# Grouped attentions of a four-layer transformer kernel: the pair of scores goes to TensorE ahead of the pair of transposed scores

## The reference, cut to what matters

```
scores = einsum('hbqd,hbkd->hbqk', q, k) / sqrt(16)     # causal ones: -inf above the diagonal
p = softmax(scores, axis=-1)
a = einsum('hbqk,hbkd->hbqd', p, v)
```

## Time and profile before

| | |
|---|---|
| median of 3 runs | 1981.44 us |
| the profiled execution, its own time | 1984.31 us |
| its span in the trace | 1982.5 us |
| granted TensorE clock, mean | 0.925 of 2.4 GHz |
| TensorE (PE) busy | 1670.2 us, 84% |
| VectorE (DVE) busy | 1185.9 us, 60% |
| ScalarE (ACT) busy | 977.1 us, 49% |
| GpSimd (POOL) busy | 471.6 us, 24% |

### The profile page before, as it was taken

How to read it: one execution, slowest core, us unless ns; L and a number is a source line. 1 busy time by engine, 2 the same in 40 slices (tenths; PEclk the granted TensorE clock), 3 DMA queues, 4 the chain that set the end, 5 groups by cost and what they waited for, 6 DMA issues and landing times. The chain is left out here.

```text
span 1982.5 us, 29923 instructions
## 1 busy us (share of the span) xinstructions
PE 1670.2 (84%) x10912; PEld 1007.5 (51%) x10912; DVE 1185.9 (60%) x2606; ACT 977.1 (49%) x1547; POOL 471.6 (24%) x546
## 2 busy tenths in 40 slices
PE   5899999989999999931289999869998999998676
PEld 2455555568865565511145555546775344433443
DVE  3576767442335665649857666446444677775376
ACT  1677879732323555533025445536663366566322
POOL 5120210022323223011132321015664323210100
PEclk9899999999998999975589999978999899999698
DMA  6342240010043355010155325031112354140322
GB/s 205 78 96 49 65 94 4 1 64 0 0 126 105 97 149 149 2 49 0 40 149 149 95 74 132 1 121 48 49 49 83 90 149 136 46 117 1 115 85 86
DMA packets 67045, 156.16 MB, mean 79 GB/s; under 512 B 9869, under 2 KB 15382, under 8 KB 66010
## 3 DMA queue, kind: packets, MB, share of 16 engines
q1 hardware_dynamic: 66906, 154.32, 27.8%
HBM read 104.86 MB, written 51.52 MB: 79 GB/s over the span
## 5 line engine op out<-in xcount | busy, mean ns | idle before, releaser
L995 DVE TENSOR_REDUCE a_mx<-PS 128x1 f32<-128x512 f32 (+3 forms) x768 | 394.5, 552 | 195.1 <-PE PS L1237 118.5
L1178 ACT ACTIVATE a_pT<-PS 128x1024 f32<-128x1024 f32 (+3 forms) x384 | 308.7, 811 | 221.9 <-PE PS L1261 152.9
L1232 PE MATMUL PS<-a_k,a_q 64*128 64x512 f32 (+3 forms) x768 | 231.1, 420 | 34.3 <-DVE a_mx L995 24.5
L367 DVE CUSTOM_DVE_ANT_0 PS<-PS,a_dist 128x448 f32<-128x448 f32 x256 | 155.1, 648 | 73.7 <-PE PS L598 72.8
L1252 PE MATMUL PS<-a_q,a_k 64*128 64x512 f32 (+3 forms) x768 | 176.8, 440 | 12.0 <-DVE a_q L1000 6.2
L1275 PE MATMUL PS<-a_pT,a_va 128*32 128x512 f32 (+3 forms) x1536 | 168.6, 511 | 6.0 <-ACT a_raw L1136 6.0
L1232 PEld LDWEIGHTS PS<-a_k,a_q 64*128 64x128 f32 x768 | 107.4, 190 | 107.4 <-DVE a_mx L995 88.2
L498 ACT ACTIVATE a_p<-PS,a_negm 128x448 f32<-128x448 f32 (+1 forms) x256 | 149.2, 639 | 2.5 <-DVE a_negm L367 0.7
L608 PE MATMUL PS<-cst,a_p 128*128 128x128 f32 x1024 | 145.1, 285 | 4.7 <-DVE a_pT L376 2.0
L122 PE MATMUL PS<-cst 128*128 128x512 f32 x202 | 104.4, 647 | 43.9 <-PEq L66 36.7
L1252 PEld LDWEIGHTS PS<-a_q,a_k 64*128 64x128 f32 x768 | 78.5, 188 | 113.9 <-issue 88.3
(11 more groups left out here) (344 smaller groups left out, 3461.3 us busy)
## 6 DMA issues: line engine op xcount, KB each, us to landing
spread_scratch<-a_high SPq DMA_DIRECT2D x96, 256.0 KB, 7.1
a_q<-spread_scratch SPq DMA_DIRECT2D x96, 256.0 KB, 5.7
a_k<-spread_scratch SPq DMA_DIRECT2D x96, 256.0 KB, 6.6
f_gb<-gate_rows SPq DMA_DIRECT2D x68, 256.0 KB, 5.4
spread_scratch<-a_low SPq DMA_DIRECT2D x48, 256.0 KB, 7.5
window_scratch<-a_high SPq DMA_DIRECT2D x24, 256.0 KB, 2.3
a_q<-window_scratch SPq DMA_DIRECT2D x32, 192.0 KB, 5.8
a_k<-window_scratch SPq DMA_DIRECT2D x32, 192.0 KB, 6.3
```

The lines of the kernel that those rows point to most:

```text
L367: dve.tensor_tensor_reduce(PS[:, bank, 0:KW], PS[:, bank, 0:KW], dt_[:, off:off + KW], float(slopes[2 * pair + a]), 3e38, ALU.add, ALU.min ...
L995: dve.tensor_reduce(mx[:, gg % 2, qt, 2 * half + a:2 * half + a + 1], PS[:, 4 + a, 0:kw], AX.X, ALU.max).then_inc(max_done, 1)
L1178: act.activation(pT[:, N // 2 % 2, N % 2, :, q0:S], PS[:, 2 * (N % 2):2 * (N % 2) + 2, q0:S], ACT.Exp, scale=SCALE).then_inc(exp_done, 1)
L1232: mm = pe.matmul(ps[:, 0:kw], q[rows, b % 2, pair, qt * P:(qt + 1) * P], k[rows, b % 2, pair, 0:kw], start=True, stop=not causal)
```

## The change

In the loop over N of TensorE's order the pair of `scores` is put ahead of `scores_T(N)`. Nothing else is changed; no instruction, wait or buffer is added or removed, and the other engines keep their orders.

```diff
@@ -1357,10 +1357,10 @@
                 for u in range(NU):
                     pe.wait_ge(unit_low[u], 1)
                 for N in range(FULL):
-                    scores_T(N)
                     for t in (2 * N + LEAD, 2 * N + LEAD + 1):
                         if t < NB * TILES_:
                             scores(t)
+                    scores_T(N)
                     if N % 2 and N >= 3:
                         values((N - 3) // 2)
                     piece(*piece_at(N), previous_piece(N))
```

## The result

The changed kernel took 1991.14 us, the median of 12 runs (1986.11 to 2002.83), and before, run beside it 12 times, 1976.55 us (1970.60 to 1983.08): the ratio is 1.008 with a 95% interval of 1.0058 to 1.0101, so 14.6 us slower. The forecast was a sum of +14.5 us. The total is right, in part by luck: of its four terms two hold and two are too large, and a gain and many small costs that I had not seen make up the difference.

What follows compares the result with a forecast made beforehand. TensorE was taken to bound the attentions, in a ring of waits with VectorE. Terms 3.8 + 4.0 + 3.7 + 3.0 = +14.5 us on 1981.44 gave 1996 us; range for 8 in 10, 1974 to 2012.

Steps and rivals of the forecast that it cites:

- The ring: Scores, VectorE's reduction, scores after next in the same bank: same work as before in attention 3, so worth nothing.
- The copy of the finished group: Values after N % 8 = 2 wait for ScalarE's copy, 0.24 us later in 16 of 28 groups: +3.8 us.
- The division: At N % 8 = 3 VectorE's division delays the reduction; 0.30 lost less 0.14 gained, in 25 groups: +4.0 us.
- The rotations: Attention 2's twelve rotated pieces hold VectorE; transposed pairs of 0.24 to 0.40 us land behind the wait: +3.7 us.
- The widths: Behind the copy of the maxima, N % 8 = 0 gets a narrower filler, 0.16 us in 19 groups: +3.0 us.
- theory B: The experiments' alternative: the order costs inside TensorE, some 38 ns in each of 384 steps, whatever other engines do.
- No change: Rival: part of each transposed pair behind a wait is hidden by early weight loads; 1986 us, within 0.5%; chance 0.25.
- Slower by more: Rival: reductions gain nothing from earlier scores; 82 waits of 0.30 us, +28.4 in all, 2010 us; chance 0.14.
- Faster: Rival: scores fill the waits for copies of the maxima at N % 8 = 0; -12.5 us, 1969 us; chance 0.13.
- The signs named: Trace marks: copy 2.1 us behind prior step's start; attentions 1, 2, 3 longer by 4, 8, 1 or 2 us.

Runs made afterwards that it cites:

- all three away: Changed order against old order, both with equal widths, copy ahead of the exponential, division put off where the next step has no piece: 1981.22 against 1975.66 us.
- swap_odd: Against the kernel before, scores go ahead of transposed scores in odd steps only: 2023.39 us, ratio 1.0239.
- copy_first_after: Changed kernel with ScalarE's copy of the finished group ahead of the exponential at N % 8 = 2: 1984.41 us, ratio 1.0051 to before.

## Why the prediction was right, and where not

**The ring.** Right in the main: VectorE's waiting for scores is unchanged (183.4 and 181.6 us), and attention 3, where all widths are equal, lost 2.5 us of the 16.1.

**The copy of the finished group** (predicted 3.8 us): about 4.6 us, the fall at place 3 just told. The traces give it directly too. In the same 16 groups as before the values start 0.14 us behind the copy, and they now start later behind the first instruction of the step before: by 0.24 us in 9 groups, as forecast, by 0.37 in 6 and by 0.64 in one, together 5.0 us. One of the six is in steps 26 and 27 of attention 1, after the change:

```profile
662.33 0.46 PE L1232 MATMUL PS<-a_k,a_q 64*128 64x128 f32 x2
662.59 0.41 PE L1252 MATMUL PS<-a_q,a_k 64*128 64x384 f32 x1
...
663.29 0.81 ACT L1178 ACTIVATE a_pT<-PS 128x768 f32<-128x768 f32 x1 [0.18 <-PE PS L1261]
...
664.00 0.59 ACT L1136 ACTIVATE a_raw<-PS 128x512 f32<-128x512 f32 x1
...
664.73 1.06 PE L1275 MATMUL PS<-a_pT,a_va 128*32 128x512 f32 x8 [0.61 <-ACT a_raw L1136]
```

The values start 0.14 us behind the copy as before, but 2.40 us behind the step's first instruction, against 2.03: 0.37 and not 0.24. The second tile of scores was held a little and kept the transposed pair back: in these six groups it starts 0.14 us behind the first, in the nine others 0.01 (the one with 0.64 lies in a stretch at 1.2 GHz). I had taken the pair's cost from a step where nothing was held.

**The division** (predicted 4.0): the step failed in its size. Steps 27 to 29 after the change:

```profile
666.32 0.50 PE L1232 MATMUL PS<-a_k,a_q 64*128 64x512 f32 x2
...
666.72 0.42 DVE L1011 TENSOR_TENSOR a_at<-PS,a_rs 128x256 f32<-128x256 f32 x1
666.75 0.37 PE L1252 MATMUL PS<-a_q,a_k 64*128 64x256 f32 x2
667.06 2.06 DVE L995 TENSOR_REDUCE a_mx<-PS 128x1 f32<-128x512 f32 x3
...
667.79 0.50 PE L1232 MATMUL PS<-a_k,a_q 64*128 64x512 f32 x1 [0.57 <-DVE a_mx L995]
```

The order is as forecast: scores, division, reduction, wait. But the reduction starts at 667.06, 0.08 us ahead of the division's end at 667.14: VectorE overlaps the start of one instruction with the end of the last. I had set it 0.00 to 0.02 behind, though the earlier trace rows already show such an overlap of 0.08 us (the second product ends at 1116.23, the reduction starts at 1116.15). From the start of the division's second half to the held scores it is now 1.07 us (666.72 to 667.79), before 1.32 (667.67 to 668.99); so 0.25 us are won against the 0.30 lost, not 0.14. The interval that begins at place 4 grew in the typical group of attention 1 by 0.05 us (1.425 to 1.477), not 0.16. Over the three attentions place 4 has 0.56 + 0.57 + 1.74 = 2.9 us, more than half of it in attention 3: there seven intervals grew from 1.25 to 1.48 us, and the one behind each became 0.11 shorter (2.36 to 2.25), -0.85 us at place 5. Net that is 2.0 us and not 4.0. No run takes the division away by itself.

**The rotations** (predicted 3.7): attention 2 lost 1.8 us more than attention 1, and 2.8 more in the pairs with equal widths and with all three away. The uncovered pairs cost what was forecast. Behind the four pieces of a batch the intervals grew by 0.41 (1.37 to 1.78, forecast 0.40), 0.36 (1.29 to 1.65, forecast 0.36) and twice 0.30 (1.75 to 2.05), of which attention 1 has 0.06 and 0.11 too (forecast 0.24). The step that failed is that all of this is lost: right in front of the 0.41, the interval that holds the piece at N % 32 = 7 fell from 3.58 to 3.17 us.

**A gain that was left out.** This is of a kind that my sum does not have. The piece behind a turning of maxima waits until the copies of the maxima have left bank 7. Now the transposed pair of the same step stands in front of that wait and fills it. Step 23 of attention 1 shows it, before and then after:

```profile
656.86 0.41 PE L1232 MATMUL PS<-a_k,a_q 64*128 64x384 f32 x1
...
657.12 1.23 DVE L1000 TENSOR_SCALAR a_q<-PS 16x1024 fp32r<-16x1024 f32 x1
...
658.50 0.36 PE L1217 MATMUL PS<-a_w_highv,a_xnT 128*128 128x256 f32 x1 [0.24 <-DVE a_q L1000]
```

```profile
655.42 0.44 PE L1232 MATMUL PS<-a_k,a_q 64*128 64x384 f32 x1
...
655.71 1.23 DVE L1000 TENSOR_SCALAR a_q<-PS 16x1024 fp32r<-16x1024 f32 x1
...
655.80 0.30 PE L1252 MATMUL PS<-a_q,a_k 64*128 64x128 f32 x1
...
657.09 0.36 PE L1217 MATMUL PS<-a_w_highv,a_xnT 128*128 128x256 f32 x1
```

In both the piece starts 0.15 us behind the copy's end and 1.64 or 1.67 us behind the scores, now with a transposed pair in between, and the interval fell from 3.63 to 3.26 us. Before, line 1217 stood 1.5 us in 6 such places and line 1207 0.7 us in 3, after the change in none. At about 0.4 us each the nine places won some 3.5 us (an estimate from these intervals), so it was wrong that all terms have the same sign.

**The widths** (predicted 3.0): with equal widths the cost fell from 16.1 to 13.2 us, 2.9, by the intervals alone.

**What was missing.** 16.1 - 4.6 - 2.9 - 1.8 - 2.0 = 4.8 us are in none of the terms, and six of the nine gains just told, some 2.2 us, are in this remainder too, so that the small costs are about 7 us. With all three terms away attention 1 still loses 1.7 us in 115 steps, 15 ns in each on average; most of its intervals at places 0, 1, 2 and 4 grew by 0.01 to 0.04 us. That much of theory B may stand. I did not find its cause. These costs made up for the terms that were too large, so that the sum came out closer than its parts: luck.

**The rivals.** No change (the early weight load): the held tile of scores in the steps above has its load together with it again (both at 667.79), and the whole sum is there. Slower by more: refuted for the same reason as said, VectorE is mostly free when the scores come. Faster: at N = 16, 48 and 80 of attentions 1 and 2 the waits for ScalarE's copy (0.57 to 0.66 us) are gone and waits of line 1232 stand in their place, 13.1 us in 31 places at N % 8 = 0 over the three attentions, before none; the intervals that end there did not get shorter (1.75 to 1.98 and 2.10 both). At N = 0 this rival did act. There the wait for VectorE's copy fell from 2.01 to 0.87 us, and the scores of step 1 start 1.26 us earlier behind the last tile in front of the loop (attention 1: 3.25 and 4.51 us). At step 8 nothing of it is left: its first instruction starts 19.10 and 19.11 us behind that tile.

**The signs named.** The copy was to end 2.1 us behind the first instruction and ends 2.13 behind it in 9 of the 16 groups, 2.26 in most of the others. Attention 1 was to lose about 4 us and lost 5.9; attention 2, 8 and 7.7; attention 3, 1 to 2 and 2.5.

## What to carry to other kernels

In a hand-ordered loop whose engines wait for each other in rings, moving one block past another costs little in a ring that keeps its contents (2.5 us in attention 3); look for the pairs of instructions between which something new now stands, for waits that the moved block used to fill, and for waits that it fills now. Price such a place from both timelines: what is uncovered behind the wait, less what the waited-for engine wins by starting earlier, where that engine's consecutive instructions may overlap. And where a short copy on a third engine stands behind a long operation that it does not need, put it in front: that gave 6.8 us in the old order, while no order by itself was faster than before, and only with it did an order with two fillers in one window win 11 us.

## What the runs showed of the hardware that I had not expected

The executions of one kernel differ by TensorE's granted clock, averaged over the run: for the changed kernel 1986.11 us at 0.930, 1990.25 at 0.928, 1994.94 at 0.924, 2002.83 at 0.919. A line through the runs of all kernels, each about its own mean, has a slope of -1.3 us for 0.001 of clock. Short stretches at 1.2 GHz fall in different places of the attentions in different executions.

TensorE was kept standing more in swap_odd, and it had less clock: the median over its four runs is 0.9135, that of before, run beside it, 0.928. Its profiled execution:

```profile
core 0: 2025.4 us, clock 0.908
```

By that slope the difference of 0.0145 is worth 19 us of the 49 that it lost; the intervals that lie outside stretches at 1.2 GHz in both traces account for 20.6, and some 10 are in neither. So in this kernel the lower clock went with about as much time again as the waits themselves. That the waits lower the clock is not shown: copy_first_after, which waits less than the changed kernel, had less clock too (0.9226 and 0.9252). For the changed kernel itself the clock is a small part at most: 0.9252 on average, before 0.9267 in 18 runs of another series, which is 2 us.
